# A new software pipeline over attention pairs on one core: values two steps behind, projection three, one shared PSUM bank

## What is computed

```python
proj = other @ W1 + readout @ W2 + b ; h = gelu(proj)
x = layernorm(h)
q, k, v = x @ qkv_w.T                       # 16 heads of 64
attn = softmax(q @ k.T * 64**-0.5 + bias)   # bias: 32 relative buckets per head
h = h + (attn @ v) @ o_w.T
x = layernorm(h)
h = h + (silu(x @ wg.T) * (x @ wu.T)) @ wd.T   # 256 to 768 to 256, integer weights / 127
```

## Time and profile before

| | |
|---|---|
| median of 3 runs | 2022.75 us |
| the profiled execution | 2022.72 us |
| its span, first to last instruction | 2020.9 us |
| mean granted TensorE clock | 0.988 of full speed |
| busy: TensorE, VectorE, ScalarE, GpSimd | 93%, 86%, 72%, 44% of the span |
| chain that ended last, by engine | TensorE 57%, VectorE 19%, ScalarE 18%, issue 3% |

### The profile page before, as it was taken

The page is one execution under the profiler, slowest core; times in us unless marked ns, Lnnn a source line. Parts: engine busy times, 40 slices in busy tenths (PEclk is TensorE's granted clock), DMA queues, the critical chain, the costliest instruction groups (busy, mean ns, idle before and its releaser), DMA issues.

```text
span 2020.9 us, 42647 instructions
## 1 busy us (share of the span) xinstructions
PE 1883.2 (93%) x15402; PEld 1713.2 (85%) x15402; DVE 1735.1 (86%) x5248; ACT 1464.1 (72%) x4034; POOL 883.4 (44%) x1103
## 2 busy tenths in 40 slices
PE   3699999999999999999999999999999999999995
PEld 1588888888888888888888888888888888888884
DVE  3488998888898889898889899888889888889884
ACT  5577777777777777777777777777777777777773
POOL 0254444444444444444444444444444444444441
PEclk9799999999999999999999999999999999999998
DMA  6000000000000000000000000000000000000000
GB/s 206 30 1 14 14 10 14 14 14 7 14 9 14 14 15 6 14 12 11 15 14 6 14 14 9 14 14 15 7 14 9 14 15 14 6 14 13 3 7 11
DMA packets 24887, 34.36 MB, mean 17 GB/s; under 512 B 2449, under 2 KB 17810, under 8 KB 24674
## 3 DMA queue, kind: packets, MB, share of 16 engines
q1 hardware_dynamic: 15202, 20.03, 3.4%
q10 hardware_dynamic: 8704, 8.36, 1.3%
q0 software_dynamic: 768, 3.21, 0.4%
HBM read 23.17 MB, written 8.42 MB: 16 GB/s over the span
## 4 chain that ended last, share of the span: by engine, by line
PE 57%; DVE 19%; ACT 18%; issue 3%; POOL 0%; DMA 0%; SPq 0%; POOLq 0%; DVEq 0%
PE ps L455 32%; PE ps L512 8%; PE ps L523 7%; PE ps L502 7%; ACT prob L695 6%; DVE prob L839 4%; PE ps L465 3%; DVE hT L882 2%; DVE pT L849 2%; DVE gate L873 2%; ACT L695 2%; ACT L671 2%; DVE heads L859 2%; ACT pT L702 2%; DVE gated L877 2%
## 5 line engine op out<-in xcount | busy, mean ns | idle before, releaser
L432 POOL TENSOR_TENSOR prob<-prob,inv 128x510 f32<-128x510 f32 x512 | 530.3, 1038 | 795.3 <-DVE inv L854 795.2
L695 ACT ACTIVATE prob<-prob,neg_top 128x255 f32<-128x255 f32 x1024 | 509.6, 502 | 55.7 <-DVE neg_top L839 55.2
L702 ACT ACTIVATE pT<-ps 128x512 fp32r<-128x512 f32 x512 | 277.9, 594 | 241.9 <-PE ps L512 241.9
L455 PE MATMUL ps<-xnT,wqk 128*128 128x256 f32 x3072 | 424.9, 287 | 1.4 <-DVE xnT L814 1.4
L455 PEld LDWEIGHTS ps<-xnT,wqk 128*128 128x128 f32 x3072 | 378.7, 189 | 2.5 <-DVE xnT L814 1.8
L839 DVE CUSTOM_DVE_ANT_0 prob<-ps,bias 128x255 f32<-128x255 f32 x1024 | 370.6, 418 | 9.9 <-PE ps L502 8.3
L849 DVE TENSOR_TENSOR pT<-ps,pT 128x512 fp32r<-128x512 f32 x512 | 328.5, 683 | 1.8 <-ACT pT L702 1.8
L512 PE MATMUL ps<-ident,prob 128*128 128x128 f32 x2048 | 280.4, 280 | 35.3 <-DVE heads L859 31.7
L523 PE MATMUL ps<-pT,v 128*128 128x256 f32 x2048 | 294.2, 286 | 0.3 <-DVE pT L849 0.3
L512 PEld LDWEIGHTS ps<-ident,prob 128*128 128x128 f32 x2048 | 219.8, 141 | 76.1 <-DVE heads L859 55.0
L523 PEld LDWEIGHTS ps<-pT,v 128*128 128x128 f32 x2048 | 270.7, 189 | 8.1 <-DVE pT L849 0.5
(11 more groups left out here) (89 smaller groups left out, 2632.5 us busy)
## 6 DMA issues: line engine op xcount, KB each, us to landing
xt<-x_cols SPq DMA_DIRECT2D x32, 256.0 KB, 2.6
r_rows<-readout_rows SPq DMA_DIRECT2D x32, 128.0 KB, 3.1
out<-h ACTq DMA_DIRECT2D x32, 128.0 KB
out<-h ACTq DMA_DIRECT2D x32, 127.0 KB
flipped<-bias_rows POOLq DMA_DIRECT2D x1, 3072.0 KB, 17.5
staged<-w_qk SPq DMA_DIRECT2D x8, 256.0 KB, 6.0
staged<-w_v SPq DMA_DIRECT2D x4, 256.0 KB, 8.1
staged<-w_o SPq DMA_DIRECT2D x4, 256.0 KB, 3.3
```

The lines of the kernel that those rows point to most:

```text
L432: pool.tensor_tensor(pr, pr, by, ALU.mult).then_inc(prob_done, 1)
L455: mm = pe.matmul(dst, lhs(a, k), rhs(b, k), start=(start and n == 0), stop=(stop and n == last), skip_group_check=skip)
L695: ex = act.activation(pr, pr, ACT.Exp, bias=neg_top[:, g, hh, t:t + 1], scale=-1.0, accum_out=total[:, g, hh, t:t + 1])
L702: act.activation(pT[:, hh, 0].rearrange("p k q -> p (k q)"), ps[:, bank_t[hh], :], ACT.Copy).then_inc(pT_hi, 1)
```

## The change

The step counter G now runs over all pairs of all batches (256 of them, and four more steps). TensorE's step is: queries and keys of G+1, scores of G, an early block, values times probabilities of G-2, projection of G-3, transposes of G-1, a late block. The other engines' programs are rewritten in the same way. The parts:

- Values times probabilities write into one bank of their own, `bank_a`, beside each other. `bank_t` holds transposes only.
- `bank_f` is the one bank of all early and late blocks, but for the last batch. Each user waits until the one before has been read (`gated_done`, `v_lo`, `lnT_lo`, `pre_done`, `out_done`).
- The tokens are one block in step 0. The down projection of batch i-2 is one block of six steps in step 1 of i (`hT` has six buffers). Gate/up of i-1 is spread over steps 4 to 7, the second norm is in step 4, the first norm of i+1 in step 6.
- The low part of the hidden tile is made on GpSimd (`gated_lo`), the high part of the second norm on ScalarE. There is one inverse per pair instead of two.
- `xt` has three buffers and holds the gelu's result too (`h0` is gone). `oT`, `tanh_g` and `gated` have two.
- The stores go to SP's queue. The output of i-2 is formed in step 1 of i, the residual of i-1 in step 2 of i, both in `h1`.
- The last batch's gate/up, down and output follow after the loop (`finish`).

The tables, SP's order, GpSimd's `gated_lo` and step, then the steps of TensorE, ScalarE and VectorE, in this order:

```diff
-        GU_EARLY, GU_LATE = {4: 1, 5: 2, 6: 4}, {3: 0, 5: 3, 6: 5}
-        GU_BANK = (bank_d, bank_f, bank_f, bank_s[1], bank_f, bank_s[1])
+        V_GROUP = ((1, 0), (0, 0), (0, 1), (1, 1))
+        V_EARLY, V_LATE = {0: 0, 3: 3}, {1: 1, 2: 2}
+        GU_EARLY, GU_LATE = {5: 1, 7: 4}, {4: 0, 5: 2, 6: 3, 7: 5}
...
+                def store(batch):
+                    sp.wait_ge(out_done, count(1, batch))
+                    sp.dma_start(out[batch, 0:P, :], h1[:, 0, :]).then_inc(out_free, 16)
+                    sp.dma_start(out[batch, P:S, :], h1[0:S - P, 1, :]).then_inc(out_free, 16)
...
+                for i in range(B + 1):
+                    if i + 1 < B:
+                        sp.wait_ge(pre_done, count(1, i))
+                        if i >= 2:
+                            sp.wait_ge(h1_done, count(1, i - 2))
+                        load(i + 1)
+                    if i >= 2:
+                        store(i - 2)
+                store(B - 1)
...
+                def gated_lo(batch, m):
+                    pool.wait_ge(h_hi, count(MT, batch, m))
+                    pool.tensor_tensor(hT[:, m, 1, :], gated[:, m % 2, :], hT[:, m, 0, :].bitcast(F32),
+                                       ALU.subtract).then_inc(h_lo, 1)
...
+                def step(G, i, g, prev, nxt):
+                    if pair(G - 1):
+                        normalise_probs(*pair(G - 1))
+                    if i > 0 and g == 3:
+                        layer_norm(1, i - 1)
+                    if nxt and g == 2:
+                        layer_norm(0, i + 1)
+                    if gu_at(G - 1, GU_EARLY):
+                        gated_lo(*gu_at(G - 1, GU_EARLY))
+                    if gu_at(G - 1, GU_LATE):
+                        gated_lo(*gu_at(G - 1, GU_LATE))
+                    if pair(G - 2):
+                        heads_split(*pair(G - 2))
...
+                def step(has_lo, G, i, g, prev, nxt):
+                    def early():
+                        if g == 0 and i < B:
+                            if i >= 2:
+                                pe.wait_ge(gated_done, count(MT, i - 2, MT - 1))
                             values(i, 0)
+                        if g == 1 and i >= 2:
+                            if nxt:
+                                pe.wait_ge(pre_done, count(1, i + 1))
+                            elif i < B:
+                                pe.wait_ge(v_lo, count(4, i, 0))
+                            else:
+                                pe.wait_ge(gated_done, count(MT, i - 2, MT - 1))
+                            down(i - 2, has_lo)
+                        if g == 3:
+                            if i < B:
+                                pe.wait_ge(v_lo, count(4, i, 2))
+                                values(i, 3)
+                        if g == 4 and prev:
+                            pe.wait_ge(v_lo, count(4, i, 3))
+                            norm_transposed(1, i - 1)
+                        if g == 5 and prev:
+                            pe.wait_ge(gated_done, count(MT, i - 1, 0))
+                            gate_up(i - 1, 1, has_lo)
+                        if g == 6 and nxt:
+                            if prev:
+                                pe.wait_ge(gated_done, count(MT, i - 1, 2))
+                            else:
+                                pe.wait_ge(v_lo, count(4, i, 3))
+                            norm_transposed(0, i + 1)
+                        if g == 7 and prev:
+                            pe.wait_ge(gated_done, count(MT, i - 1, 3))
+                            gate_up(i - 1, 4, has_lo)
+                    def late():
+                        if g == 0 and nxt:
                             pe.wait_ge(v_lo, count(4, i, 0))
+                            tokens(i + 1)
+                        if g == 1 and i < B:
+                            if i >= 2:
+                                pe.wait_ge(out_done, count(1, i - 2))
+                            else:
+                                pe.wait_ge(pre_done, count(1, i + 1))
+                            values(i, 1)
+                        if g == 2 and i < B:
                             pe.wait_ge(v_lo, count(4, i, 1))
                             values(i, 2)
+                        if g == 4 and prev:
+                            gate_up(i - 1, 0, has_lo)
+                        if g == 5 and prev:
+                            pe.wait_ge(gated_done, count(MT, i - 1, 1))
+                            gate_up(i - 1, 2, has_lo)
+                        if g == 6 and prev:
                             if nxt:
+                                pe.wait_ge(lnT_lo[0], count(1, i + 1))
+                            else:
+                                pe.wait_ge(gated_done, count(MT, i - 1, 2))
+                            gate_up(i - 1, 3, has_lo)
                         if g == 7 and prev:
+                            pe.wait_ge(gated_done, count(MT, i - 1, 4))
+                            gate_up(i - 1, 5, has_lo)
+                    if pair(G + 1):
+                        pe.wait_ge(qk_lo, count(PAIRS, *pair(G)))
+                        queries_keys(*pair(G + 1))
+                    if pair(G):
+                        scores(i, g)
+                    early()
+                    if pair(G - 2):
+                        if pair(G - 3):
+                            pe.wait_ge(o_added, count(PAIRS, *pair(G - 3)))
+                        values_probs(*pair(G - 2))
+                    if pair(G - 3):
+                        bb, gg = pair(G - 3)
+                        if gg == 0 and bb > 0:
+                            pe.wait_ge(h1_done, count(1, bb - 1))
+                        project(bb, gg)
+                    if pair(G - 1):
+                        probs_transposed(*pair(G - 1))
+                    late()
...
+                def step(G, i, g, prev, nxt):
+                    if pair(G - 1):
+                        exps(*pair(G - 1), 1)
+                    if gu_at(G - 1, GU_LATE):
+                        tanh(*gu_at(G - 1, GU_LATE))
+                    if v_at(G - 1, V_LATE):
+                        values_hi(*v_at(G - 1, V_LATE))
+                    if g == 1 and nxt:
+                        gelu(i + 1)
+                    if pair(G - 2):
+                        probs_hi(*pair(G - 2), 1)
+                    if gu_at(G - 1, GU_EARLY):
+                        gated_hi(*gu_at(G - 1, GU_EARLY))
+                    if pair(G + 1):
+                        queries_keys_hi(*pair(G + 1))
+                    if gu_at(G - 1, GU_LATE):
+                        gated_hi(*gu_at(G - 1, GU_LATE))
+                    if v_at(G, V_EARLY):
+                        values_hi(*v_at(G, V_EARLY))
+                    if g == 4 and prev:
+                        norm_hi(1, i - 1)
+                    if gu_at(G, GU_EARLY):
+                        tanh(*gu_at(G, GU_EARLY))
+                    if g == 6 and nxt:
+                        norm_hi(0, i + 1)
+                    if pair(G):
+                        exps(i, g, 0)
+                    if pair(G - 2):
+                        heads_moved(*pair(G - 2))
+                    if pair(G - 1):
+                        probs_hi(*pair(G - 1), 0)
...
+                def step(G, i, g, prev, nxt):
+                    if pair(G - 2):
+                        probs_lo(*pair(G - 2), 0)
+                    if g == 1 and nxt:
+                        pre_gelu(i + 1)
+                    if pair(G - 1):
+                        inverse(*pair(G - 1))
+                    if g == 3 and i > 0:
+                        layer_var(1, i - 1)
+                    if gu_at(G - 1, GU_LATE):
+                        gating(*gu_at(G - 1, GU_LATE))
+                    if v_at(G - 1, V_LATE):
+                        values_lo(*v_at(G - 1, V_LATE))
+                    if pair(G - 2):
+                        probs_lo(*pair(G - 2), 1)
+                    if g == 1 and nxt:
+                        add_bias(i, g)
+                        layer_sums(0, i + 1, token_tile(i + 1), gelu_done)
+                        queries_keys_lo(*pair(G + 1))
+                    else:
+                        if pair(G + 1):
+                            queries_keys_lo(*pair(G + 1))
+                        if pair(G):
                             add_bias(i, g)
+                    if g == 1 and i >= 2:
+                        output(i - 2)
+                    if g == 1 and nxt:
+                        layer_var(0, i + 1)
+                    if g == 2 and i > 0:
+                        residual(i - 1)
+                    if v_at(G, V_EARLY):
+                        values_lo(*v_at(G, V_EARLY))
+                    if g == 3 and i > 0:
+                        normalise(1, i - 1, h1)
+                    if g == 4 and prev:
+                        norm_lo(1, i - 1)
+                    if gu_at(G, GU_EARLY):
+                        gating(*gu_at(G, GU_EARLY))
```

(74 more changed lines are left out.)

371 lines of the change are left out of this document (106 added, 265 removed).

## The result

The changed kernel took 1975.71 us (median of four runs, 1974.91 to 1975.86) against 2022.09 us for the kernel before (four runs). The ratio is 0.9767, with a 95% interval from 0.9750 to 0.9783: 46 us faster. The forecast was 1948 us in a range from 1922 to 1994; the direction and the range held, and the gain was 46 us where 75 were forecast.

The account below looks back on a forecast made before the run. TensorE's blocks, interrupted by chains that leave and return within one step, were taken as the bound. The period falls from 59.93 to 57.5 us (56.7+0.3+0.4+0.2); 31 batches save 75 us from 2022.7, giving 1948 us, range 1922 to 1994.

Parts of the forecast that it names:

- The floor: TensorE's blocks of one batch at their start-to-start prices, without any waiting: 56.7 us per batch.
- small delays: Allowance per batch for delays the hand-made queue layout misses: 0.2 us, bounds 0 and 1.3.
- Step 3: TensorE waits for the low part of values block 2, late behind VectorE's residual, statistics and variance: 0.3 us per batch.
- Step 5: TensorE waits for the gating of hidden block 0, late behind VectorE's normalisation of step 4: 0.4 us per batch.
- The sum: New period per batch, TensorE's blocks plus two late hand-overs and an allowance: 56.7+0.3+0.4+0.2, given as 57.5 us.
- The output wait: VectorE's residual in step 2 waits 0.4 to 1.0 us for the store; costed at nothing, bounds 0 and 1.5.
- Rival B: The store's wait holds step 2 by 1.5 us or more, TensorE idles in step 3: 1994 us, chance 0.15.
- Rival D: The loop through ScalarE and VectorE is the bound, not TensorE: period 59.0, near 1990 us, chance 0.13.
- rival C: Common bank's hand-overs each come 0.25 us late, making the kernel slower than before: 2056 us, chance 0.08.
- fourteen hand-overs: Users of the common bank per batch, each passing it on with 1.0 us to spare; twelve were expected in time.
- Start and end: Filling and draining the deeper pipeline outside the repeated batches: taken as 0, bounds -6 and +8 us.
- VectorE's relief: Hidden tile's low part leaves VectorE for GpSimd, 3.9 us per batch; VectorE's busy time falls by some 150 us.

Follow-up runs that it names:

- the third run: Kernel after the change, with VectorE's first-norm normalisation moved from the end of step 4 to behind the early gating of step 5: 1960.20 us.
- the run with 31 rows: Kernel after the change, plus a third store of 31 rows into a spare tensor, on which the residual waits too: 2044.58 us.
- the three edits together: Kernel after the change, with the 127-row store cut into 112 and 15, variance ahead of the inverse, normalisation behind the early gating: 1927.25 us.

## Why the prediction was right, and where it was off

The direction, the mechanism and the range were right, and the point was 28 us low. By its steps:

- **The floor**: 56.7 us forecast. With both waits taken off the period is 57.0, and the version without them runs at 57.11. The queries and keys behind the token block take 1.69 us (1006.23 to 1007.92) instead of 1.49, and the down block 2.93 instead of 2.82. The 0.2 us added for small delays covers all but 0.1 of this, 3 us.
- **Step 3, the term that was mis-sized**: 0.3 us forecast, 0.95 measured, 20 us in all. The prediction took every VectorE instruction at its length in the trace before, where the variance never took more than 0.19 us (the longest of its 64), and laid the queue out without asking what GpSimd does at that moment. The run with the variance ahead of the inverse gives 0.8 us back. The 0.15 us that are left there are what the queue's order costs, for which 0.3 was forecast, so most of the measured wait has a cause that the prediction did not have.
- **Step 5**: 0.4 forecast, 0.49 measured, 3 us in all, with the cause as stated (the normalisation in front of the gating); the third run takes it away.
- **The sum** 56.7+0.3+0.4+0.2 is 57.6 and 57.5 was used; that is 3 us of the miss. The forecast's own range, 1922 to 1984, is said to hold the bounds of the two ends and does not: with -6 and +8 us it is 1917 to 1993.
- **The output wait**: 0.4 to 1.0 us on VectorE and no cost to TensorE was forecast; 0.55 us and no cost was measured, with the period unchanged when it went. There was hardly any slack left behind it, as the run with 31 rows shows. Rival B's condition, a wait of 1.5 us or more, did not come; its price was real, since at a wait of 1.92 us 1.25 more reached TensorE.
- **Rival D** is out by the three edits together, **rival C** (the common bank) by the marks: of fourteen hand-overs the two that were laid out as late carry one.
- **Start and end**: 0 forecast, 0.7 us gained. In them is the last residual's wait of 5.9 us for a store, which the forecast named and did not price by itself; 2.8 us of it go when the store lands sooner.
- **VectorE's relief** was stated as busy time and has no term of its own in the sum. The run with the low part back on VectorE puts 21 us of the 46 on that pass. VectorE's busy time fell by 143 us (150 forecast). GpSimd's rose by 107 where 140 were forecast, though the pass itself takes the 139.5 us that it was said to: its multiplications and its casts take 10 us less each (530 to 520, 116 to 106), and what is left of the difference was not looked into.
- **What was luck**: the result lies in the range, but had the variance been held twice as long, some 25 us more, it would not have been, and nothing in the prediction spoke of that wait.

That the deeper pipeline makes the rest of the gain was argued and not run: neither the distance of the values and the projection nor the single inverse was undone by itself.

## What to carry to other kernels

When an in-order pipeline is laid out anew, read the wait that ends last at each block start and ask what the engine behind it was doing; one short instruction in the wrong place of a queue cost 26 us here. Put small copies and tensor_scalars of VectorE where GpSimd is idle, for instance ahead of the instruction that releases it. Before a piece of work goes to another engine, look at what it stands behind there and how soon its result is used: the same move gave 21 us in one order and cost 315 in the other.

## What the runs showed of the hardware

- VectorE's instruction on 128x2 numbers (the variance, a tensor_scalar) took 0.17 us alone and 0.97 us when it started 0.1 us after a GpSimd multiplication on 128x510; tensor_tensor, copy and tensor_scalar ended with GpSimd's instruction, the reciprocal did not wait.
- A store of 127 rows landed 7.4 us after the output in the kernel before, where the sixteen DMA engines were busy at a mean share of 0.07, about one of them, and 7.8 us after it in the kernel after (1012.70 to 1020.5). Cut into 112 and 15 rows, with the other edits, the run ended 2.9 us after the last output was complete (1922.61 to 1925.5), before that 8.1 us (1965.87 to 1974.0).
- Where TensorE waited 2.1 us in each batch, the period was 60.9 instead of 59.7 us in 21 of 28 batches, with the granted clock at 0.66 in the 5 us looked at; where it waited 6.3 us, the next block took 2.93 us instead of 1.67 in all four batches looked at, and the mean clock was 0.936. Waits of 0.9 us left the granted clock of the batches at 1.00.
